# Middle phase of a two-layer kernel: each engine's list of a step reordered, eleven steps, two PSUM banks for keys and values, square root's table loaded ahead

## The reference

```python
x = x + gb * experts0(h)                       # weighted sum of each token's 2 expert rows, times the gate
h = _layernorm(x, axis=-1) * (1 + ca) + sa
Q = x @ wq.T + bq                              # here x is h; K and V alike
h = jnp.maximum(x @ wi1.T + bi1, 0.0)
importance = (h @ wi2.T + bi2)[..., 0]
_, top_idx = jax.lax.top_k(importance, k)      # k = 76 of 256 keys per sequence are kept
```

## Time and profile before

| | us |
|---|---|
| median of 3 runs | 1257.17 |
| lowest and highest | 1253.78 and 1260.73 |
| span of the profiled execution | 1253.0 |
| middle phase in it, 695.4 to 780.8 | 85.4 |

### The profile page before, as it was taken

How to read it: one execution, slowest core, us unless ns; L and a number is a source line. 1 busy time by engine, 2 the same in 40 slices (tenths; PEclk the granted TensorE clock), 3 DMA queues, 4 the chain that set the end, 5 groups by cost and what they waited for, 6 DMA issues and landing times. The chain is left out here.

```text
span 1253.0 us, 40088 instructions
## 1 busy us (share of the span) xinstructions
PE 1015.2 (81%) x16123; PEld 806.7 (64%) x16123; DVE 803.2 (64%) x1631; ACT 787.4 (63%) x1728; POOL 779.9 (62%) x807
## 2 busy tenths in 40 slices
PE   6788999999999865798776387899965579999980
PEld 4567777777777754597665133566544569988870
DVE  6577878888878849210001476698876827767775
ACT  5355556565556544686565554577755579998983
POOL 6576687687677510577777310788850068888865
PEclk9889999999999987799999679799997789999995
DMA  4733232222221034311112500300016321111117
GB/s 130 163 60 54 56 53 54 53 56 55 50 54 25 5 84 136 86 52 53 52 52 52 139 0 1 73 6 6 7 3 195 126 74 46 46 45 47 43 33 207
DMA packets 120839, 79.31 MB, mean 63 GB/s; under 512 B 44144, under 2 KB 111120, under 8 KB 120528
## 3 DMA queue, kind: packets, MB, share of 16 engines
q1 hardware_dynamic: 111568, 58.12, 20.3%
q0 software_dynamic: 9088, 18.63, 5.1%
HBM read 58.15 MB, written 17.76 MB: 61 GB/s over the span
## 5 line engine op out<-in xcount | busy, mean ns | idle before, releaser
L2122 ACT ACTIVATE act_x_m<-ps_h_x_m,fc_bias_x_m 128x256 f32<-128x256 f32 (+1 forms) x480 | 185.2, 470 | 67.0 <-PE ps_h_x_m L2061 61.0
L2061 PE MATMUL ps_h_x_m<-x_T_x_m,fc_x_m 128*128 128x256 f32 (+1 forms) x960 | 205.7, 365 | 4.4 <-ACT x_T_x_m L2130 2.3
L1027 ACT ACTIVATE probT<-ps_t 128x512 f32<-128x512 f32 (+1 forms) x208 | 118.6, 594 | 143.0 <-PE ps_t L855 141.8
L2233 POOL DMA_INDIRECT x_rows_x_m<-h_dram,token_m x142 | 140.3, 988 | 96.5 <-POOLq L1756 57.0
L2061 PEld LDWEIGHTS ps_h_x_m<-x_T_x_m,fc_x_m 128*128 128x128 f32 x960 | 167.1, 196 | 24.2 <-issue 6.5
L2243 POOL DMA_INDIRECT y_dram<-y_x_m,dest_m x142 | 142.2, 1001 | 47.8 <-issue 40.3
L2080 PE MATMUL ps_o_x_m<-proj_x_m,act_x_m 128*128 128x128 f32 x1136 | 144.6, 279 | 32.7 <-DVE y_x_m L2168 26.1
L2080 PEld LDWEIGHTS ps_o_x_m<-proj_x_m,act_x_m 128*128 128x128 f32 x1136 | 133.8, 193 | 42.1 <-ACT act_x_m L2122 28.5
L777 POOL TENSOR_TENSOR rel_y<-rel_raw,own_rows 128x1024 f32<-128x1024 f32 x64 | 130.5, 2042 | 25.1 <-ACT rel_raw L1035 25.1
L957 DVE TENSOR_REDUCE neg_max<-ps_s 128x8 f32<-128x512 f32 (+1 forms) x64 | 95.5, 1492 | 70.7 <-PE ps_s L840 70.5
L2168 DVE TENSOR_TENSOR y_x_m<-ps_o_x_m,out_rows_m 128x256 f32<-128x256 f32 (+1 forms) x40 | 15.8, 395 | 164.1 <-DMA y_dram<-y_x_m,dest_m 120.9
(11 more groups left out here) (310 smaller groups left out, 2136.6 us busy)
## 6 DMA issues: line engine op xcount, KB each, us to landing
q_spread<-q_dram SPq DMA_DIRECT2D x256, 64.0 KB
got_m<-y_dram SPq DMA_DIRECT2D x32, 256.0 KB, 5.2
h_dram<-h_rows_m SPq DMA_DIRECT2D x16, 256.0 KB, 2.3
x_rows_x_m<-h_dram,token_m POOLq DMA_INDIRECT x142, 2.6
y_dram<-y_x_m,dest_m POOLq DMA_INDIRECT x142, 2.3
x<-L_attn_x SPq DMA_DIRECT2D x8, 256.0 KB, 4.1
q_dram<-qT SPq DMA_DIRECT2D x8, 256.0 KB, 12.3
gates<-gate_dram SPq DMA_DIRECT2D x16, 128.0 KB, 4.3
```

Of the source, the lines that this page charges most:

```text
L1027: act.activation(probT[to:to + n, store(m, ch), :, (2 * j + s) % 4, :], ps_t[row:row + n, t % 2, :].rearrange("p (g c) -> p g c", g=GROUPS ...
L2061: m = pe.matmul(ps_h[:, l, g, f % 2, 0:w], fc[:, slot, l, f * P:(f + 1) * P], x_T[:, slot % 2, 0:w], start=True, stop=True)
L2122: m = act.activation(out[:, slot % 2, f, 0:w], ps_h[:, l, g, f % 2, 0:w], ACT.Tanh if l else ACT.Gelu, scale=0.5 if l else 1.0, bias=fc_bi ...
L2233: pool.indirect_dma_start(out=x_rows[:, slot, h, :], out_offset=None, in_=k.h_dram, in_offset=bass.IndirectOffsetOnAxis(ap=r.token[:, c:c ...
```

## The change

The helpers do the same arithmetic on the same data. What changes:

- The loops have NCH + 3 = 11 steps.
- PE does all five groups of matmuls of chunk i-2, then the transposes of chunk i-1, then the columns of chunk i-2.
- ACT's order in a step: `weigh(i+1)`, `rectify(i-2)`, `deviation(i-1)`, `queries(i-2)`, `normalize(i-1)`, `importance(i-2)`, `modulate(i-1)`. One `weigh` instead of two stands ahead of the loop.
- DVE's order in a step: `statistics(i-1)`, `weigh(i)`, `invert(i-1)`, `rank(i-3)`, then both halves of the keys and values of chunk i-2. No `weigh` and no wait for the weights stand ahead of the loop.
- `ps_kv` has two banks, one for each half g, and PE waits for the same half of the chunk before.
- ACT runs one 128x1 square root (`warm`) ahead of everything in the phase, so the table load comes there.

```diff
--- before.py
+++ after.py
@@ -1103,9 +1103,10 @@
         imp_row = sb("imp_row", [P, NTOK])
         imp_col = sb("imp_col", [P, NT])
         compared = sb("compared", [P, 4, T])
+        warm = sb("warm_m", [P, 1])
         ps_out = ctx.enter_context(nc.psum_tensor("ps_out1", [P, CH], F32))
         ps_q = ctx.enter_context(nc.psum_tensor("ps_q1", [P, CH], F32))
-        ps_kv = ctx.enter_context(nc.psum_tensor("ps_kv1", [P, CH], F32))
+        ps_kv = ctx.enter_context(nc.psum_tensor("ps_kv1", [P, 2, CH], F32))
         ps_i = ctx.enter_context(nc.psum_tensor("ps_i1", [P, CH], F32))
         ps_col = ctx.enter_context(nc.psum_tensor("ps_col1", [P, CH], F32))
         part = ctx.enter_context(nc.psum_tensor("ps_part1", [P, 2, 4, C], F32))
@@ -1119,7 +1120,7 @@
         q_copied, kv_copied, hid_copied, imp_copied = sem("q_copied1"), sem("kv_copied1"), sem("hid_copied1"), sem("imp_copied1")
         col_turned, col_ready, ranked, bq_ready = sem("col_turned"), sem("col_ready"), sem("ranked"), sem("bq_ready")
         block = ctx.enter_context(nc.Block())
-        STEPS = NCH + 5
+        STEPS = NCH + 3
 
         def chunk(n):
 
@@ -1177,9 +1178,9 @@
                 pe.matmul(ps_q[:, :], w_T[:, 0:C], hT[:, n % 2, :], start=True, stop=True).then_inc(q_ready, 1)
 
             def keys_values(n, g):
-                wait(pe, kv_copied, 2 * n + g)
+                wait(pe, kv_copied, 2 * (n - 1) + g + 1)
                 for j in range(2):
-                    m = pe.matmul(ps_kv[:, j * 2 * C:(j + 1) * 2 * C], hT[:, n % 2, (2 * g + j) * P:(2 * g + j + 1) * P],
+                    m = pe.matmul(ps_kv[:, g, j * 2 * C:(j + 1) * 2 * C], hT[:, n % 2, (2 * g + j) * P:(2 * g + j + 1) * P],
                                   w_T[:, C:3 * C], start=True, stop=True)
                 m.then_inc(kv_ready, 1)
 
@@ -1197,23 +1198,21 @@
 
             for i in range(4):
                 pe.transpose(ps_q[:, i * C:(i + 1) * C], a.w_rows[:, i, :], k.ident[:, :])
-            pe.transpose(ps_kv[:, 0:C // 2], a.wi1_rows[:, :], k.ident[0:C // 2, 0:C // 2]).then_inc(w_turned, 1)
+            pe.transpose(ps_kv[:, 0, 0:C // 2], a.wi1_rows[:, :], k.ident[0:C // 2, 0:C // 2]).then_inc(w_turned, 1)
             for i in range(STEPS):
-                if i == 3:
+                if i == 2:
                     pe.wait_ge(w_copied, 3)
                     pe.wait_ge(wi2_ready, 1)
-                if chunk(i - 3):
-                    hidden(i - 3)
-                    queries(i - 3)
                 if chunk(i - 2):
-                    to_columns(i - 2)
-                if chunk(i - 4):
-                    columns(i - 4)
-                if chunk(i - 3):
-                    keys_values(i - 3, 0)
-                    importance(i - 3)
-                if chunk(i - 3):
-                    keys_values(i - 3, 1)
+                    hidden(i - 2)
+                    queries(i - 2)
+                    keys_values(i - 2, 0)
+                    importance(i - 2)
+                    keys_values(i - 2, 1)
+                if chunk(i - 1):
+                    to_columns(i - 1)
+                if chunk(i - 2):
+                    columns(i - 2)
 
         @block.scalar
         def _(act):
@@ -1261,26 +1260,28 @@
                 act.wait_ge(imp_ready, n + 1)
                 act.activation(imp_row[:, n * CH:(n + 1) * CH], ps_i[:, :], ACT.Identity, bias=a.bi2[:, 0:1]).then_inc(imp_copied, 1)
 
+            act.activation(warm[:, :], k.eps[:, 0:1], ACT.Sqrt)
             act.wait_ge(w_turned, 1)
             act.activation(w_T[:, :], ps_q[:, 0:3 * C], ACT.Copy).then_inc(w_copied, 1)
             act.activation(a.wo_T[:, :], ps_q[:, 3 * C:4 * C], ACT.Copy).then_inc(w_copied, 1)
-            act.activation(wi1_T[:, :], ps_kv[:, 0:C // 2], ACT.Copy).then_inc(w_copied, 1)
+            act.activation(wi1_T[:, :], ps_kv[:, 0, 0:C // 2], ACT.Copy).then_inc(w_copied, 1)
             weigh(0)
-            weigh(1)
             act.wait_ge(bq_ready, 1)
             for i in range(STEPS):
-                if chunk(i - 3):
-                    rectify(i - 3)
-                    queries(i - 3)
+                if chunk(i + 1):
+                    weigh(i + 1)
                 if chunk(i - 2):
-                    modulate(i - 2)
-                if chunk(i + 2):
-                    weigh(i + 2)
-                if chunk(i - 3):
-                    importance(i - 3)
+                    rectify(i - 2)
                 if chunk(i - 1):
                     deviation(i - 1)
+                if chunk(i - 2):
+                    queries(i - 2)
+                if chunk(i - 1):
                     normalize(i - 1)
+                if chunk(i - 2):
+                    importance(i - 2)
+                if chunk(i - 1):
+                    modulate(i - 1)
 
         @block.vector
         def _(dve):
@@ -1319,7 +1320,7 @@
             def keys_values(n, g):
                 u = 2 * n + g
                 dve.wait_ge(kv_ready, u + 1)
-                dve.tensor_tensor(a.kv[:, 2 * u:2 * u + 2, :], ps_kv[:, :].rearrange("p (j c) -> p j c", j=2),
+                dve.tensor_tensor(a.kv[:, 2 * u:2 * u + 2, :], ps_kv[:, g, :].rearrange("p (j c) -> p j c", j=2),
                                   view(a.bkv[:, :], 0, [[0, 2], [1, 2 * C]]), ALU.add).then_inc(kv_copied, 1)
 
             def rank(n):
@@ -1339,21 +1340,18 @@
 
             dve.tensor_scalar(wi2_rep[:, :], k.ones[0:C // 2, :], a.wi2[:, 0:1], None, ALU.mult).then_inc(wi2_ready, 1)
             dve.tensor_scalar(a.bq[:, :], a.bq[:, :], QK_SCALE, None, ALU.mult).then_inc(bq_ready, 1)
-            dve.wait_ge(w_copied, 3)
-            weigh(0)
             for i in range(STEPS):
-                if chunk(i - 4):
-                    keys_values(i - 4, 1)
-                if chunk(i - 5):
-                    rank(i - 5)
-                if chunk(i - 3):
-                    keys_values(i - 3, 0)
                 if chunk(i - 1):
                     statistics(i - 1)
-                if chunk(i + 1):
-                    weigh(i + 1)
+                if chunk(i):
+                    weigh(i)
                 if chunk(i - 1):
                     invert(i - 1)
+                if chunk(i - 3):
+                    rank(i - 3)
+                if chunk(i - 2):
+                    keys_values(i - 2, 0)
+                    keys_values(i - 2, 1)
 
 
 FLAT = 4 * KEPT
```

## The result

The changed kernel takes 1243.16 us (median of 6 runs, 1236.37 to 1246.62), the kernel before 1255.62 (6 runs, 1251.50 to 1260.73). The forecast time was 1246.5. The ratio is 0.9915, 95% interval 0.9888 to 0.9943: 0.85% faster, which is 10.7 us of 1256 with an interval of 7 to 14 us; the two medians alone lie 12.5 us apart. The forecast gain was 10.7 us. In a second comparison, on other runs, the same kernel came to 0.9909 (0.9869 to 0.9950). The profiled execution has a span of 1240.1 us; its device time was 1242.04.

A forecast was written before the change was run, and what follows sets the result against it. Bound: a loop of waits through PE, ACT and DVE in the middle phase. Gains of 1.46 (opening), 6.95 (seven steps) and 2.26 (end) sum to 10.7 us: span 1242.3, carried to the median 1246.5 us; range 1242 to 1254.

The forecast's parts named there:

- The loop: Middle phase, each old step: normalize, transposes, keys and values, and DVE's list close a loop of waits, 8.6 us a step.
- The second bank: Keys and values: PE fills one bank while DVE reads the other, so PE does not wait; no separate price.
- The opening: Start of the middle phase: early table load and freed `shift` let chunk 0's hidden layer start 1.46 us earlier.
- First step: From hidden layer of chunk 0 to that of chunk 1: 8.8 us, two matmul pairs at the low clock.
- PE's period: Steady step when PE sets it, hidden layer to hidden layer: 7.09 us.
- DVE's period: Steady step when DVE sets it: 7.57 us, 1.08 of it `shift` stalled by POOL's gate; bound in steps with `weigh`.
- The clock: TensorE's granted clock in the middle phase: expected at 1.00 from the first step on.
- rival 1: TensorE's clock falls in the steps: one fall costs about 4 us, 1250.5 us (0.15); two or three, about 1255 (0.09).
- Rival 2: Clock low throughout the steps: 12 us per step, net loss of 19 us, about 1277 us; chance 0.04.
- End: Last hidden layer to the phase's end: 7.95 us against 10.21, 2.26 us less, since only `rank(7)` follows.
- All of it reaches the end: Behind the middle phase: work starts at a barrier with no other input, so the whole 10.7 us shortens the span.

The follow-up runs named there:

- e4: Changed kernel with DVE's `weigh` moved behind `invert` and `rank`; middle phase 72.20 us, ratio 0.9897 to the kernel before the change.
- e1_cold: Changed kernel with the early square root taken out; middle phase 73.49 us, ratio 0.987 to the kernel before the change.
- e5: Changed kernel without POOL's gate multiplications, so its values differ; middle phase 68.35 us, single run 1242.03 us.
- e8: Changed kernel with DVE's step rearranged so POOL's gate runs beside the statistics and second keys-and-values half; phase 68.96 us, 1239.89 us, ratio 0.9866.
- e3_columns_early: Changed kernel with PE's transposes of the next chunk moved back between queries and keys and values; phase 114.4 us, ratio 1.0193.
- e6: Kernel before the change with only the early square root added; middle phase 89.21 us, ratio 1.0025.
- e7: Kernel before the change with only the second bank for keys and values added; middle phase 85.36 us, ratio 1.0022.
- e10: Changed kernel run and profiled once more, unchanged; middle phase 74.75 us.
- e9: Kernel before the change with three unread filler matmuls ahead of the transposes of chunks 2 to 5; middle phase 83.71 us, ratio 0.9991.

## Why the prediction was right, and where its steps were not

**The loop.** The reading that a step is closed through PE's transposes when they stand ahead of the keys and values is shown: moving that one call back makes the kernel slower than before (1.0193), and filling PE's pauses leaves the old step at 8.97 to 9.29 us with full clock. Not shown is that this call would be enough by itself: no run moves it alone in the old lists, and the moves in ACT's and DVE's lists and the two steps fewer were not priced apart.

**The second bank.** The text gave it one clause, that PE can fill one bank while DVE reads the other. The change needs it: without it the new lists gain nothing (86.31 us). The sum was right because it assumed the bank; it gave no price for it, and the expectation that did (6 us) had half of the true one.

**The opening.** Forecast 1.46, measured 1.62, but the step named the wrong cause. It subtracted the table load from the path; without the early load the opening is the same, 13.33 us. The move of `weigh(3)` behind the first `std` made the room; this is read from the lists and the load at 702.22, and no run moves it alone. In the old list, where there is none, the early load does bring 1.53 us. I had cited the Trainium skill ("ScalarE: Activation LUTs", What ACT_TABLE_LOAD costs) for 1.38 us of drain behind a load. In the changed kernel the next activation starts at 691.95, 0.02 us behind the load's end at 691.93: the trace does not agree, as in the kernel before.

**First step.** Forecast 8.80, measured 8.09 and, in the second profile, 9.11. Its length hangs on when the clock rises: in the first profile already the keys and values ran fast, in `e4` (9.31) they still took 1.91 us. The term scatters by 1 us.

**PE's period.** Forecast 7.09, measured 6.65: mis-sized by 0.44. I took the spacings from the tail of the old phase, where the columns stand between the queries and the keys and values. In the new order hidden(n) to the transposes is 4.94 us (749.80 to 754.74), not 5.23, and from there to the next hidden layer 1.71, not 1.86; the last chunk's step was at this bound of 6.65. The second step was forecast by PE too, 7.09 us, and measured 7.13, but this is luck: PE waited 0.27 us for `normed` there, and what set the step was DVE's chain. `x(2)` starts at 711.22 and hidden(2) 8.03 us behind it, as hidden(3) stands 8.04 behind `x(3)` at 718.76; the forecast had 8.13 for this distance. Over the seven steps the misses are -0.71, 0.04, 0.04, 0.29 (the three steps with 7.57 together) and -0.44, in all -0.8 us.

**DVE's period.** Forecast 7.57, measured from `x` to `x` 7.54, 7.57, 7.87, 7.57 and 7.57, the 7.87 with the low clock beside it. The stall of 1.08 us beside the gate is there in five of the eight chunks. This is the term that decided, and that `weigh` and `invert` keep their place was the right thing to look for.

**The clock.** "1.00 from the first step on" was wrong for 3 us; the queries of 727.98 ran at the lower level. The pauses before it were 0.67 and 0.78 us with the transposes and columns between, 1.45 us together where the old late steps had 1.12. The same pair of pauses, 0.70 and 0.78 us, stands before 748.04 and 749.80, and nothing fell there. But the fall was no single accident: all three profiles with the new lists as they are and two banks (the two of the changed kernel and `e1_cold`) have one such stretch in their steps, while in `e4`, `e5` and `e8`, where PE waits at most 0.41 us for `normed` in the steps, the clock stays at 1.00 behind the first one. The warning of the Trainium skill ("TensorE: Matmul & The Clock Gate", A second HAM failure mode: psum-queue depth-cycling), that short pauses make the clock swing, is borne out by these three stretches; I had set it aside. The mechanism of rival 1 thus occurred each time, where I had given one fall 0.15, but with a price of 0.3 us on DVE's chain (7.87 for 7.57) and 0.7 us in the step of PE, not the 4 us that I had written: the stretch was short, and DVE was the bound. Rival 2, low clock in every step, did not happen here, but `e3_columns_early` shows what it looks like. That PE's short pauses are harmless, and that a fall costs half of a 6 to 10 us stretch, both failed in part.

**End.** Forecast 7.95, measured 7.76.

**What follows.** "All of it reaches the end" held within the scatter; the profiled span, forecast at 1242.3 us, was 1240.1, and would have been 1244.9 had its phase not begun 4.8 us earlier by chance. Behind the phase the clock rose 15 to 17 us after the last rank in the kernel before, in `e6`, `e7`, `e8`, `e5` and `e10`, and 20 to 22 us after it in the first profile of the changed kernel and in `e1` to `e4` and `e9`. Two stretches of the first profile after, 16 and 22 us behind the last rank, and one of the second, 16 us behind it:

```profile
780.20:782.20 2.00, 1.54 (x9) 1.07 (x6) 1.43 (x2) 0.88 (x1) 1.05 (x1) 0.50 0.00 0
786.20:788.20 2.00, 0.95 (x12) 0.84 (x8) 1.78 (x2) 1.25 (x2) 0.82 (x1) 1.00 0.15 8
```

```profile
781.40:783.40 2.00, 1.09 (x10) 1.10 (x11) 1.91 (x2) 1.25 (x2) 1.07 (x1) 1.00 0.00 0
```

The late rise lengthens the attention phase by about 2 us (its last addition to `x` starts 153.8 us behind the last rank in place of 151.7). What stands behind the middle phase lasts 472.2 to 473.6 us in the six profiles with the early rise and 474.4 to 476.0 in the six with the late one. Both occur with the same changed kernel, so the late rise is not tied to it. Whether it is more frequent with the new lists (late in five of their eight profiles, in one of four with the old ones) is not shown either way, and what decides between the two stays open. It explains 2 of the 3.7 us in the table; the others lie behind the attention phase and were not followed up.

## What to carry over

A list of instructions written out by hand has loops that no data dependency asks for: follow one chunk around the engines and ask of each wait whether it is the value or only the place that is late. Reordering and buffering are one edit, since the new order moves the moment at which a buffer comes free: try each corner before crediting either. When a sum has two candidate bounds close together, as PE's 6.65 and DVE's 7.57 here, the next gain is in the list of the second engine, and a stall inside it (1.08 us of `shift` behind a gate) is cheaper to remove than any of its work.

## What the hardware showed that I had not expected

- The table load is not held by the semaphore wait of the activation that needs it: at 702.22 it ran before the moments were there and hid in that wait.
- Which DVE instructions the gate on POOL holds up: `shift` (0.16 to 1.24 us) and `x` (0.69 to 1.74 us, in the openings of the kernel before and of `e6` and `e9`), both with two SBUF tensors as inputs. With one of two inputs in PSUM, `both` (eight in 2.20 us in `e9`, half of them beside the gate) and `kv` (two in 1.28 us in `e4`) kept their durations beside it, and so did the statistics (0.86 us in `e8`).
- A pause of TensorE in a closed loop costs twice: once itself and once by the matmuls behind it. With pauses of 3.43 us the clock averaged 0.60 and the step went from 10.8 (reckoned at full clock) to 13.75 us; with 2.10 us of matmuls put into its pauses the old order held 1.00 behind its first step.
- The clock's low stretches scatter from run to run by one microsecond in the phase's first step and by some 2 us in the phase behind it, in kernels with the same instructions.
